# Issuing each unit's scores first in TensorE's step, in the first attention of a four-layer decoder

## The reference

```python
q, k, v = split_heads(x @ Wq), split_heads(x @ Wk), split_heads(x @ Wv)
# 1: softmax over 8 compressed blocks of 16 tokens
logits_c = where(c_ok, q . k_c / scale, NEG);  out_c = softmax(logits_c) @ v_c
# 2: softmax over the tokens of the 4 best blocks of each query, causal
_, top_idx = top_k(logits_c, 4);  out_s = softmax(where(allowed, q . k_s / scale, NEG)) @ v_s
# 3: softmax over a causal window of 32 tokens back
out_l = softmax(where(wmask, q . k / scale, NEG)) @ v
out = gates[..., 0:1] * merge(out_c) + gates[..., 1:2] * merge(out_s) + gates[..., 2:3] * merge(out_l)
x = x + out @ Wo
```

## Time and profile before

| | us |
|---|---|
| median of 3 runs (lowest, highest) | 1280.98 (1279.72, 1283.1) |
| the profiled execution | 1283.22 |
| its span in the trace | 1281.3 |
| the loop of the first attention, from its first mask to its last addition to x | 71.70 to 216.3 |

### The profile page before, as it was taken

One profiled execution on the slowest core, in us unless ns is written; L12 is line 12 of the kernel. 1 busy time (PEld: TensorE's weight loads), 2 busy tenths in 40 slices (PEclk: granted clock), 3 DMA queues, 4 the chain that ended last, 5 costly groups with the idle time before them and its releaser, 6 DMA issues. The chain is left out here.

```text
span 1281.3 us, 22291 instructions
## 1 busy us (share of the span) xinstructions
PE 1014.2 (79%) x8221; PEld 764.2 (60%) x8221; DVE 772.4 (60%) x1870; ACT 655.8 (51%) x1688; POOL 337.2 (26%) x440
## 2 busy tenths in 40 slices
PE   6257877785878768789999988996789952878998
PEld 4224444353775356679976765765368840547898
DVE  4889996782424666652246655665777766863422
ACT  1168885662446646635537765774122233753433
POOL 2264542662223134310003331334310031111000
PEclk9689898885889868989999999999789985988999
DMA  7300000004354000020000000002030000000000
GB/s 245 87 1 1 2 1 18 2 1 143 99 170 171 1 1 3 1 99 1 1 2 1 2 1 1 2 2 82 31 132 1 1 1 0 2 1 2 1 1 17
DMA packets 31978, 42.46 MB, mean 33 GB/s; under 512 B 7592, under 2 KB 25632, under 8 KB 30592
## 3 DMA queue, kind: packets, MB, share of 16 engines
q1 hardware_dynamic: 30848, 38.95, 9.2%
q0 software_dynamic: 1024, 2.10, 0.5%
HBM read 35.54 MB, written 5.51 MB: 32 GB/s over the span
## 5 line engine op out<-in xcount | busy, mean ns | idle before, releaser
L1291 ACT ACTIVATE arena<-bank,w_L_ffn_b1T 128x512 f32<-128x512 f32 x128 | 86.8, 687 | 102.7 <-PE bank L1233 102.3
L1268 PEld LDWEIGHTS bank<-bufB,arena 128*128 128x128 f32 x1024 | 119.2, 192 | 2.3
L1268 PE MATMUL bank<-bufB,arena 128*128 128x128 f32 x1024 | 119.8, 276 | 0.0
L2546 ACT ACTIVATE arena<-arena 128x128 f32<-128x128 f32 x256 | 99.2, 390 | 20.0 <-DVE arena L2573 20.0
L293 POOL TENSOR_TENSOR norm_rstd<-norm_std,minus_half 128x4 f32<-128x4 f32 x24 | 25.4, 1059 | 310.6 <-DVE norm_std L288 310.5
L1328 DVE SCALAR_TENSOR_TENSOR x<-bank,gate_c,x 128x128 f32<-128x128 f32 x128 | 36.0, 344 | 116.9 <-PE bank L1268 116.6
L2557 POOL TENSOR_TENSOR arena<-arena 128x512 f32<-128x512 f32 x64 | 66.6, 1040 | 150.1 <-DVE arena L2606 150.1
L545 ACT ACTIVATE arena<-arena 128x128 f32<-128x128 f32 x256 | 80.3, 395 | 42.5 <-DVE arena L553 42.5
L1233 PE MATMUL bank<-x_high,w_low 128*128 128x512 f32 x200 | 87.0, 435 | 9.7 <-DVE w_low L1242 7.1
L1233 PE MATMUL bank<-x_high,w_high 128*128 128x512 f32 x200 | 81.6, 408 | 0.0
L1233 PE MATMUL bank<-x_low,w_high 128*128 128x512 f32 x200 | 81.6, 408 | 0.0
(11 more groups left out here) (489 smaller groups left out, 2562.3 us busy)
## 6 DMA issues: line engine op xcount, KB each, us to landing
bufB<-in_L_ffn_w SPq DMA_DIRECT2D x28, 256.0 KB
bufA<-in_L_ffn_w SPq DMA_DIRECT2D x2, 2048.0 KB, 9.9
bufB<-in_L_ffn_W SPq DMA_DIRECT2D x2, 2048.0 KB
bufB<-in_L_ffn_w SPq DMA_DIRECT2D x2, 2048.0 KB
bufA<-in_L_ffn_Wgu SPq DMA_DIRECT2D x1, 2304.0 KB, 8.8
bufA<-in_L_attn_Wqkv SPq DMA_DIRECT2D x1, 2048.0 KB, 8.7
rows<-blank SPq DMA_DIRECT2D x2, 960.0 KB, 6.8
results<-arena SPq DMA_DIRECT2D x6, 256.0 KB
```

Of the source, the lines that this page charges most:

```text
L1268: i = pe.matmul(bank[:, j * P:(j + 1) * P], h[:, f, j * P:(j + 1) * P], w2[:, u * FF + f * P:u * FF + (f + 1) * P], start=f == 0, stop=f = ...
L1291: act.activation(m["h"][k % 2][:, f, :], banks[f][:, :], ACT.Gelu, bias=b1[:, c:c + 1]).then_inc(g["hidden"].sem, 1)
L2546: o = act.activation(tile, tile, ACT.Exp, bias=b2["mn"][n % 8][:, j:j + 1], scale=-1.0, accum_out=b2["sm"][n % 8][:, j:j + 1])
```

## The change

The two lines that issue the scores of unit `step` move from the end of TensorE's step to its begin, ahead of the outputs, the turning back, the values and the turns of units further back. The waits inside `score_pe` stay as they are.

```diff
@@ -662,6 +662,8 @@
                 i.then_inc(g["block_out"].sem, 1)
 
             for step in range(32 + 9):
+                if step < 32:
+                    score_pe(pe, s, h, step, t["qT"])
                 for k in (step - 9, step - 8):
                     if k % 4 == 3 and 0 <= k < 32:
                         output_pe(pe, s, h, k // 4, W["L0_attn_Wo"][:, :], turn=k == step - 8)
@@ -689,8 +691,6 @@
                 if 0 <= k < 32:
                     turn_pe(pe, s, 2 * k, h["a"][(2 * k + 1) % 8], s["exped"](k + 1))
                     turn_pe(pe, s, 2 * k + 1, h["a"][(2 * k) % 8], s["exped2"](k + 1))
-                if step < 32:
-                    score_pe(pe, s, h, step, t["qT"])
```

## The result

The changed kernel takes 1273.62 us in the median of 12 runs, the kernel before 1281.62 in 12 runs beside it. The ratio is 0.9924 (95% interval 0.9902 to 0.9945): 9.7 us faster, between 7.0 and 12.6. The two medians themselves are 8.0 us apart, so the size of the gain is known to some 2 us only. One of the 12 runs of the changed kernel took 5156.02 us, at a granted clock of 1.00; it is counted in the median and not in the ratio. The forecast was 5.0 us. The median alone, 1273.62, would lie just inside it. The profiled execution took 1271.89 us, with a span of 1270.0.

What follows compares the result with a forecast made beforehand. VectorE was taken to bound the first attention's loop, losing time to late scores. 5.3 us of waits less 0.3 for the turning back gave 5.0 us, from 1280.98 to 1276.0 us; range 1272.8 to 1280.0.

Steps and rivals of the forecast that it cites:

- The bound: First attention's loop: VectorE is full, busy 15.86 of 16.50 us in the stretch from 99.3 to 115.8 us.
- The rewriting: TensorE's order in the loop: the edit equals issuing each score one step earlier, with everything else in the same order.
- (a): First attention's loop: VectorE's waits for scores, late behind the output product in TensorE's queue, all go; 5.3 us won.
- (b): TensorE's score now waits for the masks of one step back: 0.18 us at one close place, hidden, cost 0.
- (c): Turning back of chosen blocks' heads (L540), VectorE's next supplier, has 0.11 us in hand; 0.3 us lost over the loop.
- (d): Tail from last mask to last addition: taken as 0, up to 1.5 us more or 1 less with the clock.
- (e): After the loop the stages follow each other by data, so the gain is carried to the end.
- Gate: TensorE reaches the score before its bank is free, two score banks being too few; nothing won, 1281.0 us; chance 0.05.
- half gain: Part of the 5.3 us is absent in ordinary executions or given back later; 1 to 3.8 us won; chance 0.27.
- slower: TensorE's clock falls for long in the loop; 1288.7 us at ten such steps; chance 0.04.
- More gain: A denser loop keeps the clock up in loop and tail; 6.5 to 9 us won; chance 0.06.

Runs made afterwards that it cites:

- the fold: Gate's product (L837) folded into the unpacking: on the changed kernel, ratios 0.9845 and 0.9895 to the kernel before; on the kernel before, 0.9930.

## Why the prediction was wrong in its size

**The bound** (VectorE) was right. Its work in the loop is 124.4 us before and 123.6 after, and taking L837 out of the 16 unpackings, 0.81 us long in ten of them, shortened the changed loop by 7 us.

**The rewriting** of the edit as "each score a step earlier, all else in place" held. TensorE's order around the product is as forecast.

**(a) failed in its size**, and this is the step of the prediction that went wrong. It prices VectorE's waits for scores at 5.3 us, read from the trace of one execution as if it were a property of the kernel. The three traces list 5.4, 7.9 and 4.9 us of waits. They also cost more than their idle time shows: the masks of before exceed the 120.45 us after by 6.2, 8.7 and 5.8 us, about 0.85 more than the listed waits each time. Against the same step after the change, each step with a listed wait is 0.07 to 0.10 us longer than its wait explains. For a mask that isn't held up starts some 0.09 us before the small instruction ahead of it ends (109.04, with an L553 from 108.96 to 109.13), and the list counts only from that end. The rest stands in steps where no wait is listed: step 9 takes 4.57 us before (99.32 to 103.89) and 4.48 after (98.31 to 102.79), for in before the score (102.83, 1.02 us long) ended at 103.85, just too late, which no row counts as idle. I had the measure for this in hand, a floor from the steps without a stall, but the group that I took it from held such a short lateness itself, and I ended it with the small instruction (16.51 us; it is 16.34 after). In place of 5.3 the term is 6.9 us, the mean of the three.

**The cause in (a)** was half right. The queue in order is one part: moved ahead of values and turns, no score is late. The other part is TensorE's clock, which I had used only to argue that an execution could have less to win. At a clock of 0.99 the old order loses 1.3 us of waits, at 0.87 it loses 7.9. The output product's wait, which I named as the head of the queue, can be taken away and the loss stays.

**(b)** was right in its cost: 0.16 us at the gate, hidden. In step 14 it is 0.52, hidden as well. What it left out is the start of the loop, where the score at 76.27 was held for 2.25 us; the first masks follow each other at 3.35 us as before, so that is hidden too.

**(c)** was too careful by 0.3 us. The turning back was never late between the masks in the three traces of the changed kernel. The thin margin was real: with the fold it was late once in two traces, by 0.52 us.

**(d)** The tail is 17.9 to 19.9 us in three traces of before and 17.9 to 19.5 in three of the changed kernel. It varies by up to 2 us with the execution, about as bounded; the means differ by 0.6 us, in favour of the change, which is less than the scatter of either.

**(e)** isn't contradicted: the rest has the same mean in both within 1.1 us, with a scatter of 8.4 us between the traces of before and 3.7 between those of the changed kernel.

**The rivals.** "Gate", "half gain" and "slower" didn't come. "More gain", a denser loop with a higher clock, is what the measured 9.7 us is nearest to, and I gave it 0.06. Its mechanism is only partly so. The clock of the loop is indeed higher after (0.94, against 0.90, 0.87 and 0.90), but nothing in the changed loop is faster for it: with the clock at 0.98 its masks still take 120.46 us. What is won more, as far as the traces show it, was a larger loss before.

**Still open.** The traces account for 6.9 us in the masks and 0.6 in the tail, 7.5 us. The medians are 8.0, 7.9 and 8.8 us apart in the three comparisons, and the three ratios stand for 8.6 to 9.7 us. 7.5 lies inside each of their intervals, and the kernel before differed from itself by 1.9 us. So nothing beyond the 7.5 us is shown, and nothing rules it out: three traces of each kernel don't settle whether the loop of before is, over many executions, slower than these three show, or whether 1 to 2 us lie elsewhere.

## What to carry to other kernels

A wait read from one trace is one draw. Where a low clock made it long, look for how it varies before its size goes into a sum, and take the gain from the pitch of the steps that nothing delays, since a lateness under 0.1 us is in no list of waits. In an engine that works in order, put first what the full engine waits for: taking away the instruction behind which it all seemed to queue (here the output product) changed little, and putting the scores first in some steps left the time as it was, with waits in the steps behind.

## What the runs showed of the hardware

TensorE's clock fell after pauses of 1.6 to 2.2 us in which it waited for ScalarE, as ahead of the turns at 133.46 and, with 1.2 us of work between, ahead of those at 190.54 above, but not after each of them: behind the 1.84 us ahead of 183.20 it stayed up. One more product of 1.02 us in each step kept it up: the granted clock of the loop was 0.98 and 0.99, in two kernels, where it was 0.87 to 0.94 in the traces of the kernel before and the changed one. More work on an engine with room can so shorten a loop. The old order's masks took 4 to 7 us less with it, in one trace against three.

The small product L837, 16 values in each partition, takes 0.81 us in ten of the 16 unpackings, while GpSimd makes masked keys (L474), and 0.17 us in the last six, where GpSimd has no keys left to make. In the kernel before (VectorE and GpSimd; in step 29, from 188.61 on, GpSimd is idle):

```profile
101.69 1.04 POOL L474 TENSOR_TENSOR arena<-arena,mask 128x512 f32<-128x512 f32 x1
101.95 0.81 DVE L837 TENSOR_TENSOR arena<-arena 128x16 f32<-128x16 f32 x1
...
188.83 0.17 DVE L837 TENSOR_TENSOR arena<-arena 128x16 f32<-128x16 f32 x1
```

In three traces of the kernel before and three of the changed one each of the long L837 ends 0.02 to 0.04 us behind the end of a GpSimd instruction, so it lasts as long as what GpSimd has left to do. The Trainium skill (SBUF — State Buffer, Who interferes with whom) says that a VectorE instruction with two inputs in SBUF contends with a GpSimd instruction that reads SBUF. The durations agree with that; no run here moved the GpSimd instruction to test it.

L553, with 4 values in each partition, shows the same: 0.40 to 0.41 or 0.27 us when it ends behind a GpSimd instruction, again by 0.01 to 0.04 us, and 0.17 to 0.18 otherwise. 45 of the 64 in a loop are longer so. An estimate from these durations (32 times 0.24 and 13 times 0.10 us) is some 9 us of a loop that VectorE bounds, about what the change won. What of it could be won is untested.
